# Routed experts by halves: tiles of one expert from scattered rows, expert matrices chosen by a register

## The chip, the cores and the metric

One core of a Trainium2 chip. The metric is the device time of one execution in microseconds (us). The engines are named as in the profile: PE is TensorE, DVE is VectorE, ACT is ScalarE, POOL is GpSimd, SP is SyncE, whose instructions here are nearly all DMA issues.

## The reference

A decoder of two layers on `x` of 4 x 256 tokens x 256, float32. Layer 0 is attention with 16 heads, a graph attention over a context, and 32 masked experts of which each token takes one. Layer 1 is attention with rotary positions (16 heads, 4 key heads of 128), a cross attention, and the stage that changes:

```python
probs = softmax(xt @ w_router)                     # xt: 1024 tokens x 256, 16 experts
top_w, top_i = top_k(probs, 4);  top_w /= sum(top_w)
cw = zeros(T, 16).at[arange(T)[:, None], top_i].add(top_w)
g = silu(einsum('td,edh->teh', xt, we1)) * einsum('td,edh->teh', xt, we3)    # h = 128
moe_out = einsum('teh,ehd->td', g * cw[:, :, None], we2)
shared = silu(xt @ ws1) * (xt @ ws3) @ ws2         # hidden size 512
out = shared / 5 + moe_out * 4 / 5
x = layernorm(x + out)
```

## The kernel before

Everything stays in SBUF between stages; each stage is a block with a hand-written instruction stream per engine, and semaphores between them. Every float32 product is made as three matmuls in fp32r: an operand is kept as a rounded part (`_hi`) and the rest (`_lo`), and `mm3` (L115) adds hi*hi, hi*lo and lo*hi in PSUM.

The last block, `cross_and_experts`, has the norm behind the attention, the cross attention, norm5, the turning of x into `xt_hi` and `xt_lo` (channels on partitions), the router, and then 20 "pieces": 16 experts and four quarters of the shared expert (`PIECES`), all dense: each piece is computed for all 1024 tokens, and VectorE adds its output to `c.x`, scaled by a gate per token that is 0 for an expert not chosen (`add`). For a piece, `up` does 24 matmuls with 512 moving columns (first and third matrix, two halves of the tokens), ScalarE takes silu, VectorE the product, ScalarE the rounded part and GpSimd the rest (`low`), and `down` does 24 matmuls with 256 moving columns for eight tiles of 128 tokens. `up` of the next piece stands before `down` of the present one. SyncE loads a piece's three matrices into two buffers in turn, and GpSimd splits them in two parts (`split`, L1682 and L1684). norm6 and four stores end the kernel.

Layer 0's masked experts (`graph_and_masked_experts`) already work by sorting: `rank` and VectorE's steps behind it give each token's place in an order by expert, eight indirect DMAs on GpSimd (L1380) scatter the rows of x to DRAM, SyncE loads them back, TensorE turns them and multiplies each tile of 64 rows with the matrix of its expert, whose column comes from a register (L1440, L1441), results go to DRAM by SyncE (L1358), and eight indirect DMAs gather them (L1388).

The diff also touches the attention block, which both layers use. In it SyncE's queue is one loop over the groups g of heads, which for layer 1 (`rope`) comes to: wait for the splits of the projections of group g - 1, load `raw_q` and `raw_k` of g; wait for the split of `raw_o` of g - 1, load `raw_o` of g. GpSimd splits these weights (L398, L401) and adds the two parts of the rotated queries and keys (`rotate`, L626), in an order written out by hand; TensorE waits for these sums before a step's scores (L759). In layer 0, behind the load of `raw_o` of group 2, SyncE also writes zeros to the 3 MB of `sorted_rows` (L600).

## Time and profile before

| what | us |
|---|---|
| median of 3 runs | 902.44 (900.88 to 908.67) |
| the profiled execution, its own time | 903.48 |
| its span, first to last instruction | 901.7 |

Mean granted clock of TensorE: 0.955 of full speed. Busy shares of the span: PE 89%, DVE 64%, ACT 48%, POOL 55%; 20% for the DMA queue of SyncE's transfers. Engines work at the same time, so a share says what an engine could still take, not what its work is worth; that is read from what others wait for. The times in the rows count from the first instruction of the span.

### The profile page before, as it was taken

What the parts mean: (1) busy time and instruction counts of PE and PEld (TensorE: products, weight loads), DVE (VectorE), ACT (ScalarE), POOL (GpSimd) and SP (SyncE); (2) the same over time, 40 slices, a digit from 0 to 9 for tenths busy, and PEclk for the clock granted to TensorE, in tenths of its full rate; (3) what the DMA queues carried; (4) which work ended last, traced back from release to release, by engine and by line L of the source; (5) the groups of instructions that cost most, each with busy time, mean ns of one, the idle gap of its engine ahead of it and who ended that gap; (6) DMA issues with size and microseconds to landing.
All of it is one profiled execution on the core that took longest, in us unless ns stands there. A gap on an engine that the chain in (4) does not pass through costs nothing. (4 is left out here: it accounts for less than half of the span.)

```text
span 901.7 us, 14551 instructions
## 1 busy us (share of the span) xinstructions
PE 801.8 (89%) x4733; PEld 685.0 (76%) x4733; DVE 574.4 (64%) x1651; ACT 429.2 (48%) x1209; POOL 499.8 (55%) x411
## 2 busy tenths in 40 slices
PE   7899999999999876792789999998987599999995
PEld 5678888888888764490678888887875388888885
DVE  4696867868769466123677667876736655545545
ACT  4264635536446544162366665666663532232232
POOL 4757287556587351513455564556422367777774
PEclk8999999999999997896999999999999799999998
DMA  6220711212315112553001111011001011111111
GB/s 200 71 94 1 234 36 59 94 36 106 115 50 180 55 54 65 186 120 88 30 6 48 53 53 53 1 54 53 24 1 37 12 35 52 35 52 52 35 41 47
DMA packets 58331, 59.09 MB, mean 66 GB/s; under 512 B 5392, under 2 KB 49312, under 8 KB 58272
## 3 DMA queue, kind: packets, MB, share of 16 engines
q1 hardware_dynamic: 57504, 56.24, 20.0%
q0 software_dynamic: 768, 2.10, 0.7%
q8 instruction: 32, 0.52, 0.2%
q14 instruction: 27, 0.22, 0.1%
HBM read 50.00 MB, written 8.32 MB: 65 GB/s over the span
## 5 line engine op out<-in xcount | busy, mean ns | idle before, releaser
L889 ACT ACTIVATE a_probs<-bank,a_neg_peak 128x128 f32<-128x128 f32 (+1 forms) x256 | 103.2, 429 | 88.9 <-DVE a_neg_peak L997 88.9
L917 ACT ACTIVATE a_probs<-a_probs,a_row_inv 128x128 f32<-128x128 f32 (+1 forms) x256 | 92.0, 447 | 20.8 <-DVE a_row_inv L1005 20.7
L997 DVE CUSTOM_DVE_ANT_0 bank<-bank,causal 128x128 f32<-128x128 f32 (+1 forms) x256 | 82.3, 394 | 15.3 <-PE bank L759 15.3
L895 ACT ACTIVATE a_probs_t<-bank 128x512 f32<-128x512 f32 x96 | 53.9, 597 | 73.5 <-PE bank L779 73.5
L1700 POOL TENSOR_TENSOR d_h_lo<-d_h,d_h_hi 128x512 fp32r<-128x512 f32 x40 | 51.7, 1293 | 52.6 <-ACT d_h_hi L1819 39.0
L398 POOL TENSOR_TENSOR a_wk_hi<-raw_k,one 128x512 fp32r<-128x512 f32 (+1 forms) x24 | 21.6, 901 | 102.3 <-DMA raw_k<-in_L_attn_w_k_dram 64.1
L798 PE MATMUL bank<-a_probs_t,a_vals 128*128 128x256 f32 x256 | 76.5, 380 | 0.0
L118 PE MATMUL bank<-a_wo_hi,a_ot_hi 128*128 128x256 f32 x256 | 74.5, 291 | 0.7 <-DVE a_ot_lo L1017 0.7
L1905 DVE TENSOR_TENSOR d_h<-d_silu,bank 128x512 f32<-128x512 f32 x40 | 27.5, 688 | 72.9 <-PE bank L120 72.8
L119 PE MATMUL bank<-a_wo_lo,a_ot_hi 128*128 128x256 f32 x256 | 73.2, 286 | 0.0
L120 PE MATMUL bank<-a_wo_hi,a_ot_lo 128*128 128x256 f32 x256 | 73.1, 286 | 0.0
L1912 DVE SCALAR_TENSOR_TENSOR x<-bank,d_gate,x 128x256 f32<-128x256 f32 x160 | 64.6, 477 | 2.5 <-PE bank L120 0.2
L140 PE MATMUL bank<-idle 128*128 128x512 bf16 x98 | 32.7, 505 | 35.3 <-DVE x L1597 16.3
L118 PE MATMUL bank<-xt_hi,d_w_hi 128*128 128x512 f32 x160 | 63.9, 400 | 0.0
L120 PE MATMUL bank<-xt_hi,d_w_lo 128*128 128x512 f32 x160 | 63.9, 399 | 0.0
L119 PE MATMUL bank<-xt_lo,d_w_hi 128*128 128x512 f32 x160 | 63.9, 399 | 0.0
L765 PE MATMUL bank<-a_keys,a_queries 128*128 128x256 f32 x256 | 60.6, 379 | 0.0
L779 PE MATMUL bank<-ident,a_probs 128*128 128x128 f32 x384 | 53.4, 275 | 6.2 <-ACT a_probs_t L895 6.2
L779 PEld LDWEIGHTS bank<-ident,a_probs 128*128 128x128 f32 x384 | 44.3, 141 | 16.5 <-ACT a_probs_t L895 10.8
L626 POOL TENSOR_TENSOR a_queries<-sim 128x512 f32<-128x512 f32 x32 | 40.7, 1279 | 27.6 <-DVE sim L972 27.6
L972 DVE TENSOR_TENSOR sim<-bank,a_sin 64x512 f32<-64x512 f32 x80 | 55.0, 688 | 1.1
L889 ACT ACTIVATION_READ_ACCUMULATOR a_probs<-bank,a_neg_peak 128x1 f32 x256 | 55.3, 216 | 0.0
(316 smaller groups left out, 2429.5 us busy)
## 6 DMA issues: line engine op xcount, KB each, us to landing
d_raw<-in_L_ffn_we_dram SPq DMA_DIRECT2D x48, 128.0 KB, 2.2
raw_k<-in_L_attn_w_k_dram SPq DMA_DIRECT2D x8, 512.0 KB, 6.5
raw_q<-in_L_attn_w_q_dram SPq DMA_DIRECT2D x8, 512.0 KB, 5.7
raw_v<-in_L_attn_w_v_dram SPq DMA_DIRECT2D x8, 512.0 KB, 7.3
raw_o<-in_L_attn_w_o_dram SPq DMA_DIRECT2D x8, 512.0 KB, 3.7
kv<-_L_ffn_expert_masks_dram SPq DMA_DIRECT2D x16, 256.0 KB, 3.1
kvt<-_L_ffn_expert_masks_dram SPq DMA_DIRECT2D x16, 256.0 KB, 3.1
raw_q<-in_L_attn_Wq_dram SPq DMA_DIRECT2D x8, 512.0 KB, 4.7
```

Source lines behind the costliest of these rows:

```text
L118: nc.tensor.matmul(out, l_hi, r_hi, start=start, stop=False)
L119: nc.tensor.matmul(out, l_hi, r_lo, start=False, stop=False)
L120: return nc.tensor.matmul(out, l_lo, r_hi, start=False, stop=stop)
L765: last = nc.tensor.matmul(out, queries[:, j, row + P:row + T], keys[:, j % keys.shape[1], row:row + width], start=True, stop=True)
L779: last = nc.tensor.transpose(c.banks[3 + turned % 2][:, slot % 4 * P:(slot % 4 + 1) * P], probs[s % 2][:, i, at:at + P], c.ident[:])
L798: nc.tensor.matmul(out, vals_of(s)[:, 2 * i, cols], probs_t[:, at:at + T], start=True, stop=False)
L889: nc.scalar.activation(probs[s % 2][:, i, at:at + width], c.banks[i][:, at:at + width], ACT.Exp, bias=neg_peak[:, n:n + 1], scale=-1.0, ac ...
L895: nc.scalar.activation(probs_t[:, i * BANK:(i + 1) * BANK], c.banks[3 + (3 * s + i) % 2][:], ACT.Copy).then_inc(s_pt_free, 1)
L917: last = nc.scalar.activation(part, part, ACT.Copy, scale=row_inv[:, s % 2, n + r:n + r + 1])
L972: last = nc.vector.tensor_tensor(two(across[to:to + HALF_BLOCK, n % 2]), two(bank[at:at + HALF_BLOCK]), many(sin[at:at + HALF_BLOCK], HALF ...
L997: last = nc.vector.tensor_tensor_reduce(part, part, mask, -1.0, 3e38, ALU.add, ALU.min, neg_peak[:, n + r:n + r + 1])
L1912: last = nc.vector.scalar_tensor_tensor(c.x[:, t], c.banks[4 + u][:, (t % 2) * D:(t % 2 + 1) * D], g, c.x[:, t], ALU.mult, ALU.add, accum_ ...
```

## The change

The routed experts become sparse; the shared ones stay dense.

- Tokens are taken in two halves of 512. For each half, the four chosen experts of each token give four places in an order by expert, in which each expert begins a new tile of 128 rows. `TILES1` = (512 x 4 - 16) // 128 + 16 = 31 is the most tiles that can be needed, and always all 31 are computed, in `PAIRS1` = 16 pairs (the last has one tile).
- `scatter`: GpSimd writes x's rows to `sorted1` in DRAM with 16 indirect DMAs for a half; `load_sorted`: SyncE loads pairs of tiles; `turn`, `hidden`, `turn_hidden`, `outputs` on TensorE; `sorted_high`, `silu_of`, `hidden_high`, `evict` on ScalarE; `sorted_low`, `gated`, `hidden_low` on VectorE. The expert's matrices stay in SBUF for all 16 experts (`w`), and a tile's are found by a register loaded from `column`. `store` writes results to `y_sorted`; `gather`: 16 indirect DMAs on GpSimd for a half; `combine`: VectorE adds the four rows of a token times their gates.
- All weights are split before the first routed product: ScalarE rounds (`high`), GpSimd or VectorE take the rest (`low`); several pieces are split ahead of the router. The shared experts run by halves (8 steps) while places are found and rows are scattered.
- In layer 1's attention SyncE writes zeros to `sorted1`: 2 MB behind the load of `raw_o` in each of the groups 1 to 4.
- Memory of earlier stages is given back for the expert matrices (`early`), and semaphores of the first two blocks are cleared and used again.

The diff, cut to its core:

```diff
@@ decoder
+        c.sorted1 = [nc.dram_tensor(f"sorted_rows1_{half}", (2 * PAIRS1 * P, D), F32, kind="Internal").ap() for half in range(2)]
@@ attention, SyncE's loop over g
                     weights.load(sp, "o", g)
...
+                    if rope and g <= 4:
+                        blank = c.idle[:].bitcast(F32).unsqueeze(1).broadcast_to([P, PAIRS1, D])
+                        rows = slice((g - 1) % 2 * PAIRS1 * P, ((g - 1) % 2 + 1) * PAIRS1 * P)
+                        sp.dma_start(c.sorted1[(g - 1) // 2][rows].rearrange("(t p) d -> p t d", p=P), blank).then_inc(c.s_blank, 16)
@@ graph_and_masked_experts, SyncE, at its start
+                for sem in c.finished:
+                    sp.sem_clear(sem)
@@ cross_and_experts
+TILES1 = (HALF * TOPK - EXPERTS1) // P + EXPERTS1
+PAIRS1 = -(-TILES1 // 2)
+    ORDER = ["s0", "s1", 0, 1, 2, "s2", "s3"] + list(range(3, EXPERTS1))
...
+                for n in range(len(Pieces.ORDER)):
+                    load_piece(n)
+                for i in range(8):
+                    load_sorted(i)
+                for i in range(ALL):
+                    if i + 8 < ALL:
+                        load_sorted(i + 8)
+                    store(i)
@@ GpSimd
+                def scatter(half):
+                    pool.wait_ge(s_place, half + 1)
+                    for t in HALF_TILES[half]:
+                        for k in range(TOPK):
+                            nc.gpsimd.indirect_dma_start(c.sorted1[half], bass.IndirectOffsetOnAxis(place[:, t, k:k + 1], 0), c.x[:, t], None).then_inc(s_scattered[half], 16)
+                def gather(t):
+                    if t % (NT // 2) == 0:
+                        for i in range(4):
+                            pool.wait_ge(s_stored[i], 16 * (PAIRS1 // 4) * (t // (NT // 2) + 1))
+                    if t >= 2:
+                        pool.wait_ge(s_summed, t - 1)
+                    for k in range(TOPK):
+                        nc.gpsimd.indirect_dma_start(got[t % 2][:, k], None, y_sorted[t // (NT // 2)], bass.IndirectOffsetOnAxis(place[:, t, k:k + 1], 0)).then_inc(s_got[t % 2], 16)
                 norm4.roots(pool)
+                low(0)
+                low(1)
...
+                for n in range(2, 5):
+                    low(n)
                 norm5.means(pool)
                 norm5.roots(pool)
-                split_up(0, 0)
-                with pool.Fori(0, PIECES // 2 - 1) as i:
...
+                pool.wait_ge(s_norm5, NT)
+                for n in range(5, 8):
+                    low(n)
+                pool.wait_ge(c.s_blank, 16 * 5)
+                scatter(0)
+                for n in pieces.by_pool[8:]:
+                    low(n)
+                scatter(1)
+                for t in HALF_TILES[0]:
+                    gather(t)
+                norm6.root(pool, 0)
+                for t in HALF_TILES[1]:
+                    gather(t)
+                norm6.root(pool, 1)
@@ TensorE
+                def hidden(i, columns):
+                    pe.wait_ge(s_xs_lo, i + 1)
...
+                        for k in range(KC):
+                            hi, lo = (w_flat[:, bass.ds(columns[2 * (i % 4) + t] + (j + k) * D, D)] for j in (0, 3))
+                            last = mm3(nc, out, xs_hi[:, i % 2, k, at], xs_lo[:, i % 2, k, at], hi, lo, k == 0, k == KC - 1)
-                turned5.pe(pe, s_norm5, 4)
-                router.pe(pe, turned5)
-                up(0, 0)
...
+                turned5.pe(pe, s_norm5, 4, halves=[0])
+                router.raw_pe(pe, turned5, halves=[0])
+                turned5.pe(pe, s_norm5, 4, halves=[1])
+                router.logits_pe(pe, halves=[0])
+                up(0)
+                rank(0)
...
+                for n in range(1, STEPS1):
+                    if n + 1 < STEPS1:
+                        up(n + 1)
+                    down(n)
+                turn(0)
+                turn(1)
+                split_wait(pe, len(Pieces.ORDER) - 1)
+                for i in range(ALL + 2):
+                    if i < ALL:
+                        if i % 4 == 0:
+                            columns[i // 4] = columns_of(i)
+                        hidden(i, columns[i // 4])
+                    if 1 <= i <= ALL:
+                        turn_hidden(i - 1)
+                    if i + 2 < ALL:
+                        turn(i + 2)
+                    if i >= 2:
+                        outputs(i - 2, columns[(i - 2) // 4])
@@ ScalarE
+                for n in range(STEPS1):
+                    shared(n)
+                    if n + 8 in pieces.by_dve:
+                        high(n + 8)
+                    shared_high(n)
+                for n in pieces.by_pool[8:]:
+                    high(n)
+                for half in range(2):
+                    act.wait_ge(s_above, half + 1)
+                    nc.scalar.activation(likely[:, part_of(half)], above[:, part_of(half)], ACT.Exp).then_inc(s_likely, 1)
+                nc.scalar.activation(primed[:], c.one[:], ACT.Silu)
+                sorted_high(0)
+                sorted_high(1)
@@ VectorE
+                norm5.apply(dve, 0, s_norm5)
+                turned5.dve(dve, halves=[0])
+                norm5.apply(dve, 1, s_norm5)
+                choose(0)
+                turned5.dve(dve, halves=[1])
+                find(0)
+                shared(0)
+                shared_low(0)
+                choose(1)
+                shared(1)
+                shared_low(1)
+                find(1)
+                for n in range(2, STEPS1):
+                    shared(n)
+                    for m in LOWS_AT[n]:
+                        low(m)
+                    shared_low(n)
+                    if n == SHARED:
+                        shared_total(0)
+                shared_total(1)
...
+                AT = {PAIRS1 + 5 + 2 * j: j for j in range(NT // 2)}
+                for i in range(ALL + 1):
+                    if i < ALL:
+                        gated(i)
+                    if i >= 1:
+                        hidden_low(i - 1)
+                    if i + 2 < ALL:
+                        sorted_low(i + 2)
+                    if i in (2, 4):
+                        gates(i // 2 - 1)
+                    if i in AT:
+                        combine(AT[i])
+                aggregate(0)
+                norm6.apply(dve, 0, s_norm6)
+                for t in HALF_TILES[1]:
+                    combine(t)
+                aggregate(1)
+                norm6.apply(dve, 1, s_norm6)
```

## Rows read from the trace of the kernel before

**Rows 1.** Windows by stage: length, busy us (instructions), granted clock, DMA share, GB/s

```profile
432.00:680.00 248.00, 228.79 (x1393) 199.87 (x1392) 168.37 (x480) 150.95 (x473) 125.57 (x98) 0.99 0.10 34
...
720.80:891.90 171.10, 171.08 (x962) 148.79 (x961) 94.83 (x235) 50.72 (x83) 119.24 (x117) 0.99 0.14 40
891.90:901.70 9.80, 0.00 (x0) 0.00 (x0) 4.22 (x16) 4.04 (x16) 2.83 (x6) 0.67 0.32 107
```

**Rows 2.** Chain of waits through one piece of the experts: start us, us, what

```profile
829.78 0.24 PE bank L118
...
838.25 0.24 PE bank L118
```

**Rows 3.** Timeline of TensorE, layer 0: start us, us, engine line op, idle

```profile
383.68 0.36 PE L1440 MATMUL bank<-b_w,xt_hi 128*64 x1
...
387.42 1.03 PE L1424 MATMUL bank<-ident,spare 128*128 128x128 f32 x8
```

**Rows 4.** Groups by line in the experts: busy us, mean ns, idle before

```profile
L1905 DVE TENSOR_TENSOR d_h<-d_silu,bank 128x512 f32<-128x512 f32 x40 | 27.5, 688 | 72.9 <-PE bank L120 72.8
L1684 POOL TENSOR_TENSOR d_w_lo<-d_raw,d_w_hi 128x512 fp32r<-128x512 f32 x20 | 25.8, 1292 | 1.6
...
L1816 ACT ACTIVATE d_silu<-bank 128x512 f32<-128x512 f32 x40 | 23.9, 597 | 54.6 <-PE bank L120 53.0
...
L1821 ACT ACT_TABLE_LOAD x1 | 1.3, 1283 | 0.0
```

**Rows 5.** Timeline of VectorE, norm5's scalings by halves

```profile
707.45 1.39 DVE L1183 TENSOR_SCALAR x<-x,d_d_norm_neg_mean,d_d_norm_rstd 128x256 f32<-128x256 f32 x4 [1.79 <-POOL d_d_norm_rstd L1167]
709.54 4.85 DVE L1183 TENSOR_SCALAR x<-x,d_d_norm_neg_mean,d_d_norm_rstd 128x256 f32<-128x256 f32 x4 [0.70 <-POOL d_d_norm_rstd L1167]
```

**Rows 6.** Timeline of VectorE, start of layer 0's finding

```profile
354.82 0.19 DVE L1557 TENSOR_SCALAR b_segments<-bank 128x32 f32<-128x32 f32 x1 [1.47 <-PE bank L1414]
```

**Rows 7.** Timelines of layer 0's indirect DMAs, 354 to 425 us

```profile
358.74 1.85 POOL L1380 DMA_INDIRECT sorted_rows<-x,b_place  x1 [16.98 <-DVE b_place L1572]
...
406.75 0.57 SPq L1358 DMA_DIRECT2D y_sorted<-raw_o  x1
...
410.27 1.01 POOL L1388 DMA_INDIRECT sim<-y_sorted,b_place  x1 [8.31 <-DMA y_sorted<-raw_o]
...
419.28 1.18 POOL L1388 DMA_INDIRECT sim<-y_sorted,b_place  x1 [0.30 <-issue]
...
422.25 0.43 DVE L1595 TENSOR_TENSOR sim<-sim,rows 128x256 f32<-128x256 f32 x1 [1.71 <-DMA sim<-y_sorted,b_place]
```

**Rows 8.** Timeline of SyncE's queue in layer 1's attention

```profile
471.72 0.37 SPq L383 DMA_DIRECT2D raw_o<-in_L_attn_Wo_dram  x1
...
472.68 0.47 SPq L383 DMA_DIRECT2D raw_k<-in_L_attn_Wk_dram  x1
```

**Rows 9.** Timeline of GpSimd in layer 1's attention, group 2's splits

```profile
477.16 0.61 POOL L398 TENSOR_TENSOR a_wk_hi<-raw_k,one 128x256 fp32r<-128x256 f32 x1 [5.46 <-DMA raw_k<-in_L_attn_Wk_dram]
...
480.78 2.54 POOL L626 TENSOR_TENSOR a_queries<-sim 128x512 f32<-128x512 f32 x2
```

**Rows 10.** Timeline of TensorE, the scores behind them

```profile
483.38 1.16 PE L759 MATMUL bank<-a_keys,a_queries 128*128 128x128 f32 x8 [0.19 <-POOL a_queries L626]
```

**Rows 11.** Timelines of SyncE and GpSimd, layer 0, loads behind its blank DMA

```profile
92.92 6.71 SPq L383 DMA_DIRECT2D raw_q<-in_L_attn_w_q_dram  x1
...
108.97 1.04 POOL L398 TENSOR_TENSOR a_wk_hi<-raw_k,one 128x512 fp32r<-128x512 f32 x1 [17.04 <-DMA raw_k<-in_L_attn_w_k_dram]
```

**Rows 12.** Window within that blank DMA, columns as in rows 1

```profile
96.00:98.00 2.00, 2.00 (x14) 1.76 (x13) 1.79 (x5) 0.60 (x1) 0.00 (x0) 1.00 1.08 386
```

**Rows 13.** Timelines of GpSimd and TensorE, layer 1, behind group 4

```profile
567.60 1.29 POOL L626 TENSOR_TENSOR a_queries<-sim 128x512 f32<-128x512 f32 x1 [1.98 <-DVE sim L972]
...
572.28 1.06 PE L759 MATMUL bank<-a_keys,a_queries 128*128 128x128 f32 x8
```

**Rows 14.** Window at half the granted clock, columns as in rows 1

```profile
722.00:724.00 2.00, 2.00 (x6) 1.63 (x5) 1.78 (x20) 1.55 (x2) 0.00 (x0) 0.50 0.00 0
```

More of the change, by code:

```diff
@@ new lines, in cross_and_experts @@
+        same = sb("same", [P, NT // 2, TOPK, EXPERTS1])
+        chosen = [sb(f"chosen{h}", [P, NT // 2 + 1, EXPERTS1], BF16) for h in range(2)]
+        earlier, every = sb("earlier", [P, P], BF16), sb("every", [P, P], BF16)
+        segments, through, ones = sb("segments", [P, EXPERTS1]), sb("through", [P, EXPERTS1]), sb("ones", [P, EXPERTS1])
+        magic, primed = sb("magic", [P, 2]), sb("primed", [P, 1])
+        tile_number, tile_expert = sb("tile_number", [1, EXPERTS0]), sb("tile_expert", [1, EXPERTS0])
@@ L1723, in _, with rank @@
+                norm6.root(pool, 0)
+                for t in HALF_TILES[1]:
+                    gather(t)
+                norm6.root(pool, 1)
             @block.tensor
             def _(pe):
-                pe.sem_inc(s_out, 2 * OUT)
-                pe.sem_inc(s_up, 8)
+                def rank(half):
+                    pe.wait_ge(s_chosen, half + 1)
+                    at = (NT + half * (NT // 2 + 1)) * EXPERTS1
+                    out = router.outs[half][:, at:at + (NT // 2 + 1) * EXPERTS1]
+                    nc.tensor.matmul(out, earlier[:], flat_of(chosen[half][:]), start=True, stop=False)
+                    for t in range(NT // 2):
+                        later = NT // 2 - t
+                        last = nc.tensor.matmul(out[:, (t + 1) * EXPERTS1:], every[:], chosen[half][:, t:t + 1].broadcast_to([P, later, EXPERTS1]), start=False, stop=t == NT // 2 - 1)
+                    last.then_inc(s_rank, 1)
@@ new lines, in down @@
+                def down(n):
+                    half, name, first = n // SHARED, f"s{n % SHARED}", n % SHARED == 0
+                    if first and half:
+                        pe.wait_ge(s_total, 2)
+                    for u in range(2):
+                        if first:
+                            nc.tensor.matmul(c.banks[2 + u][:], c.ident_bf[:], c.zero[:].broadcast_to([P, BANK]), start=True, stop=False)
+                        if u == 0:
+                            pe.wait_ge(s_h_lo, n + 1)
+                        for t in range(2):
+                            cols = slice((2 * u + t) * P, (2 * u + t + 1) * P)
+                            last = mm3(nc, c.banks[2 + u][:, t * D:(t + 1) * D], h_hi[:, n % 2, cols], h_lo[:, n % 2, cols], w_hi[name][:, KC], w_lo[name][:, KC],
+                                       False, t == 1 and n % SHARED == SHARED - 1)
+                        last.then_inc(s_shared, 1)
@@ new lines, in columns_of @@
+                def columns_of(i):
+                    if i % PAIRS1 == 0:
+                        pe.wait_ge(s_column, i // PAIRS1 + 1)
+                    first = i % PAIRS1 // 4 * 8
+                    _, columns = nc.values_load_multi_w_load_instructions(column[i // PAIRS1][0:1, first:first + 8], engines=[mybir.EngineType.PE], min_val=0, max_val=(EXPERTS1 - 1) * 2 * PIECE,
+                                                                          skip_runtime_bounds_check_because="VectorE counts at least 0 experts and takes at most the last")
+                    return columns
@@ L1856, in _ @@
                 for half in range(2):
[L1857 removed]
+                    part = part_of(half)
                     dve.wait_ge(s_exp, HALF_TILES[half].stop)
@@ L1864, in _ @@
                     last.then_inc(norm5.s_sum, 1)
-                for half in range(2):
-                    norm5.apply(dve, half, s_norm5)
-                turned5.dve(dve)
-                wide = lambda v: v.broadcast_to([P, NT, EXPERTS1])
-                dve.wait_ge(router.s_logits, 1)
-                nc.vector.tensor_copy(logits[:], router.out[:, 0:NT * EXPERTS1].rearrange("p (t e) -> p t e", t=NT))
-                dve.drain()
-                for t in range(NT):
-                    nc.vector.max(best[:, t], logits[:, t])
@@ L1876, in _ @@
-                dve.drain()
-                nc.vector.tensor_tensor(above[:], logits[:], wide(best[:, :, 0:1]), ALU.subtract).then_inc(s_above, 1)
-                nc.vector.memset(best[:, :, TOPK:], 3e38)
-                dve.drain()
-                for t in range(NT):
-                    nc.vector.match_replace(others[:, t], best[:, t], logits[:, t], -3e38)
-                dve.drain()
-                nc.vector.tensor_tensor(more[:], logits[:], others[:], ALU.is_gt)
-                dve.wait_ge(s_likely, 1)
```

604 lines of the change are left out of this document (398 added, 206 removed).

## The prediction

> **What bounds the kernel now.** I read the stretches by stage first [rows 1]. Layer 1's attention takes 248.0 us; norms, cross attention and router follow, then 171.1 us of dense experts and a tail of 9.8 us. TensorE is busy 171.08 of the 171.1 us with experts, so there its own work is the bound; in the attention it is busy 228.8 of 248 and every small gap matters. The second view is the chain in the experts [rows 2]: one piece (an expert, or a quarter of the shared one) begins at 829.78 and the next at 838.25, a period of 8.47 us. In it a 512-column matmul costs 0.233 us (the steps of 0.24, 0.23, 0.23 in the chain), so a 256-column one (8.47 - 24 x 0.233)/24 = 0.12 us. A matmul's own row shows 0.28 or more, which is latency, since they overlap. Twenty pieces at 8.47 make 169 us, the stage. DMA is lightly used (40 GB/s). Third, for a part of the diff that lies outside the experts, the timelines of GpSimd, SyncE and TensorE in layer 1's attention.
>
> **Fewer tile products.** Now 16 experts x 8 tiles of 128 tokens = 128 products; each is 18432/8 = 2304 columns. The new code always does 31 tiles in each half, so 62 products of nine 256-column matmuls (2304 columns too), whatever the router says. New for each tile: three 128x128 transposes (two of the rows, one of the hidden layer). Layer 0 already works like this with registers: 32 matmuls with a register in the address run from 383.68 to 387.42, 0.117 each, and eight transposes take 1.03 with the latency of the last, so about 0.11 each; nothing is left there for the loading of eight registers [rows 3]. I take 0.119 and 0.11: 62 x 9 x 0.119 = 66.4, 62 x 3 x 0.11 = 20.5, together 87 us where 16 x 8.47 = 135.5 stood: 48.6 us less on TensorE. For two tiles ScalarE does two 256-column copies or activations and two of 512 (some 2.0 us by its 0.60 for 512 columns [rows 4]), VectorE some 1.6 us by its 0.69 [rows 4], against TensorE's 2.8, so TensorE still leads.
>
> **The start of the experts.** Now TensorE reaches its first expert matmul at 720.84. Before it, VectorE needs 4.85 us for the four scalings of norm5's second half where the first took 1.39, while GpSimd splits weights [rows 5]. The change makes GpSimd wait for norm5 and orders the work by halves: second half scaled some 711.6 to 713.0, transposes to 714, first-half logits 715. So the shared experts start at 715, 5.8 earlier. For this I take GpSimd's three lows (1.9 us each, by 1.29 for 512 columns [rows 4]) and ScalarE's highs (0.85 each) as hidden in the stretch where TensorE does nothing anyway; if they meet the two tiny VectorE scalings behind the peaks, it costs up to 4.
>
> **The shared experts, halves and finding.** Eight steps of 12 wide and 12 narrow matmuls: 12 x 0.233 + 12 x 0.119 = 4.2 us, 34 us. But choosing and finding stand on VectorE ahead of the first two products. Layer 0's finding began at 354.82 [rows 6], and its first scatter, released by the places, at 358.74 [rows 7]; by halves some 2.8, choosing 2.5, and the experts' numbers behind each place 2.0. Walked through in order this gives down(0) at 729.5, rank(1) at 732, down(2) at 741.3 and the last product's end at 762.2: 47 us. Then ScalarE has four weight copies (3.5), two table loads of 1.28 [rows 4] and two 512-column copies, and GpSimd four lows (7.8); the first routed product starts at 768.7, 6.5 us idle. Scatter of half 0: 16 issues at the 1.29 us of layer 0's indirect DMAs (410.27 to 419.28 is seven of them [rows 7]), 21 us from 725, hidden under the shared experts (without that cover it would cost all 20); that of half 1 lies under half 0's products: it ends at about 790. Two queues stand behind it: SyncE waits for it before loading half 1's rows, with the stores of results 8 and later queued behind that wait (first needed at 797, when the twelfth copy reuses its buffer), and TensorE reaches half 1 at 813. VectorE waits in its order for each gather of half 0 before later tiles' products; that is priced below.
>
> The Trainium skill, page "SBUF — State Buffer", section "SBUF: two separate sides", speaks against this: VectorE operations with two SBUF inputs can hold the port that GpSimd needs, and its descriptors starve. Rows show little of it for indirect DMAs (1.01 us alone, 1.18 beside VectorE's two-input sums [rows 7]). By the rule the eight lows of weights (1.0 us each) and eight of hidden rows (0.7) on VectorE, 13.6 us, would move the scatter's end from 746 to about 760, still ahead of 768.7, so the sum would not change.
>
> **Routed phase.** 87 us, plus 2 for a slow clock after the idle time, 2 to fill and drain the pipeline, 4 where VectorE waits for half 0's gathers (bounds 0 and 12: the first gather lands about where its sum stands in the order, and each gather of four takes 5.2 against 5.6 for two steps). Bounds for all three: 2 and 18. TensorE ends at 768.7 + 95 = 863.7, where it now ends at 891.9.
>
> **The tail.** Now 9.8 us. New, after the last matmul: copy and wait 0.8; store issued to first gather 3.5 (406.75 to 410.27 [rows 7]); 16 gathers, 15 x 1.29 = 19.3 to the last issue; landing 2.9 (419.28 to 422.25 [rows 7]); four sums 2.0; moments 1.2; root 1.6; scaling 1.4; store 2.9. Sum 35.6. GpSimd reaches half 1's gathers only behind norm6's first root, which waits for VectorE's aggregate, but that is over before the last store lands; a gather also waits for the sum of the tile two before (9 us after that tile's first issue, where 10.3 us of issues lie between). So the end is at 899.3 against 901.7: the experts by themselves give **2.4 us**. The 48.6 us of TensorE go into 13 for the shared experts' latency, 6.5 for the gap, 8 for the pipeline and 26 for the tail, with 6 back at the start.
>
> **The blank DMAs in the attention.** The diff makes SyncE write 2 MB of zeros (16 x 128 rows of 1 KB) behind the load of raw_o in groups 1 to 4 of layer 1's attention. On SyncE's queue the very next instructions are the loads of raw_q and raw_k for the next group: raw_o is issued at 471.72, raw_q directly behind and raw_k at 472.68 [rows 8]. And GpSimd stands waiting for that raw_k: 5.46 us idle to 477.16, splits, then at once the two rotations of the queries until 483.3 [rows 9]. TensorE's next scores start at 483.38, 0.19 us after it had run dry, released by exactly these queries [rows 10]. So raw_k's landing lies on the chain to TensorE, with no slack. Layer 0 shows what a blank ahead of loads does: 3 MB issued just before raw_q's load at 92.92, SyncE stuck 6.71 us in issuing raw_q, raw_k landed at 108.97, GpSimd idle 17.04 us [rows 11], while DMA ran at 386 GB/s [rows 12]. 2.1 MB at 386 GB/s is 5.4 us; layer 0's raw_k was 2.7 us later than the bytes ahead of it need (raw_o, blank, raw_q and raw_k are 4.7 MB, 12.2 us; counted from 94.0, 1.1 us behind raw_q's issue), so up to 7.2 here. I take 6. Groups 1 to 3: 3 x 6 = 18. In group 4 the rotation now waits 1.98 us for VectorE and TensorE for nothing [rows 13]: the splits would end at 571.6 instead of 565.6, two rotations at 574.15, TensorE starts 1.9 after its 572.28. Together 20 us (bounds 17.5 and 24.7). What is late next is TensorE itself, busy from there on; nothing gives the time back. After idle stretches of 4.5 us the clock's record is at half for some 3 us (0.50 at 722 to 724, in the middle of busy experts, some 8 us after the idle time that ended at 714.4 [rows 14]), where TensorE does half the work: 1.5 to 2 lost each, bounds 0 and 9 for the three, I take 6. Sum **26 us**.
>
> Costed at nothing: the clearing of some forty semaphores on SyncE, which has 22 us to wait there for TensorE's transposes; the loops written out as straight code (bounds -1 to 3, since more instructions must be fetched); 25 MB more DMA traffic below the experts (some 190 GB/s where the experts have 40 and the engines reach 386).
>
> Against the profiled execution (903.48; span 901.7 and 1.8 outside): 903.5 - 2.4 + 26 = 927.1. It was 1.0 above the median of 902.44, so 926.1; I say **926**.
>
> **Rivals.** (a) *The blanks are absorbed*, a gain being possible. For it: in layer 0 the same kind of DMA left TensorE fully busy (2.00 of 2.00 at 96 to 98 [rows 12]). Against: there TensorE did not wait on the next split. It decides by the wait in front of the scores: if it stays under 1 us, the time is 902.4 - 2.4 = 900. With the experts' terms at their cheap ends (start of routed 4 earlier, pipeline 6 less, tail 3 less) it is 887, **faster**: the rival of the other sign, decided by whether raw_k still lands near 477. (b) *The delay is there, but the experts gain as much*: shared phase at 40 instead of 47 and the cheap ends above, 926 - 20 = 906. (c) *Indirect DMAs are the bound*: if they cost 2 us each instead of 1.29, the tail grows by 11 and VectorE waits 9 more in the routed phase: 946. For it: the first scatter in layer 0 took 1.85 [rows 7]; against: the gathers took 1.01 to 1.18. (d) *The work is not halved*: 62 is fixed in the code, so this can't fail by the router's choices.
>
> **Chances.** Forecast 0.63, its own range 912 to 940; (a) near 900 0.12, (a) at the cheap end 0.08; (b) 0.09; (c) 0.08. Changes under 1% are about what a measurement of this kernel can't tell from none (893.4 to 911.5). Faster 0.10, same 0.20, slower 0.70. The range takes in (b) and half of (a): 898 to 941.
>
> **What would show it.** Waits of GpSimd for raw_k of 11 us instead of 5.5 in groups 1 to 4, and gaps of 5 to 7 us on TensorE before the scores of groups 1 to 3, 2 in the fourth; attention about 26 longer. From the end of attention on: first expert matmul some 35 us after it, last matmul some 183 after it, last gather issue 23 after that. It would be wrong if the loads overtake the blanks, if fine-grained steps leave TensorE idle between routed products (over 0.3 us each), or if scatter 0 outlasts the shared experts.

## The result and the profile after

The changed kernel took **955.53 us** (median, 954.01 to 956.52) against 903.91 for the kernel before, a ratio of 1.0565 (95%: 1.0513 to 1.0616). Slower, as forecast, but 29.5 us beyond the 926 and outside the range of 898 to 941. The profiled execution took 956.52, its span is 954.7. The three stretches that answer to [rows 1], TensorE's windows by stage (length; busy time and instructions of each engine; clock; DMA share; GB/s):

```profile
core 0: us, PE busy (x) PEld busy (x) DVE busy (x) ACT busy (x) POOL busy (x), PEclk, DMA share, GB/s
462.00:711.00 249.00, 210.61 (x1266) 185.97 (x1266) 146.87 (x421) 136.74 (x424) 111.64 (x86) 0.95 0.20 65
748.00:917.40 169.40, 141.90 (x970) 130.83 (x970) 91.18 (x236) 80.55 (x165) 60.43 (x56) 0.90 0.51 157
917.40:954.70 37.30, 0.00 (x0) 0.00 (x0) 12.65 (x32) 0.38 (x1) 17.80 (x19) 0.54 0.33 99
```

The first window holds only the last 249 us of an attention that ends at 710.99; TensorE, busy 228.8 of 248 before, is busy 210.6 here. The expert stretch, 171.08 of 171.1 busy before, has 27.5 us without work. The tail is 37.3 us.

**Attention.** The timeline of SyncE and GpSimd at the first group's end, and TensorE's first scores of the next four groups (start, duration, engine, line; in brackets the idle time before it and what ended it), which answer to [rows 8 to 10]:

```profile
470.33 0.37 SPq L394 DMA_DIRECT2D raw_o<-in_L_attn_Wo_dram  x1
470.74 0.51 SPq L615 DMA_DIRECT2D sorted_rows<-idle  x1
471.29 3.83 SPq L394 DMA_DIRECT2D raw_q<-in_L_attn_Wq_dram  x1
475.16 1.09 SPq L394 DMA_DIRECT2D raw_k<-in_L_attn_Wk_dram  x1
...
482.69 0.61 POOL L409 TENSOR_TENSOR a_wk_hi<-raw_k,one 128x256 fp32r<-128x256 f32 x1 [12.39 <-DMA raw_k<-in_L_attn_Wk_dram]
...
488.81 1.01 PE L774 MATMUL bank<-a_keys,a_queries 128*128 128x128 f32 x3 [7.00 <-POOL a_queries L641]
...
525.53 0.80 PE L774 MATMUL bank<-a_keys,a_queries 128*128 128x128 f32 x2 [6.66 <-POOL a_queries L641]
...
563.77 1.01 PE L774 MATMUL bank<-a_keys,a_queries 128*128 128x128 f32 x3 [7.79 <-POOL a_queries L641]
...
600.90 1.16 PE L774 MATMUL bank<-a_keys,a_queries 128*128 128x128 f32 x8 [2.26 <-POOL a_queries L641]
```

The blank goes first, the issue of raw_q's load is stuck 3.83 us behind it, raw_k lands late and GpSimd waits 12.39 us for it instead of 5.46; TensorE runs dry for 7 us instead of 0.19. The forecast chain, link by link. From the first raw_o issue to the end the attention takes 240.7 us (470.33 to 710.99) against 208.5: 32 more. Its price was forecast at 26.

**A hole that no step of mine had.** TensorE, ScalarE, VectorE, GpSimd and SyncE in the middle of the routed phase:

```profile
810.12 0.38 ACT L2026 ACTIVATE xt_hi<-bank 128x256 fp32r<-128x256 f32 x1 [1.05 <-PE bank L1913]
810.54 0.42 DVE L2201 TENSOR_TENSOR xt_lo<-bank,xt_hi 128x256 fp32r<-128x256 f32 x1 [1.01 <-ACT xt_hi L2026]
...
812.33 0.41 PE L131 MATMUL bank<-d_w,xt_lo 128*128 x1
812.67 0.96 POOL L1798 DMA_INDIRECT sorted_rows<-x,d_place  x1 [0.30 <-issue]
813.94 0.96 POOL L1798 DMA_INDIRECT sorted_rows<-x,d_place  x1 [0.30 <-issue]
815.04 0.36 SPq L1764 DMA_DIRECT2D d_scratch<-sorted_rows  x1
815.05 0.60 ACT L2011 ACTIVATE xt_hi<-bank 128x512 fp32r<-128x512 f32 x1 [4.54 <-issue]
815.20 0.96 POOL L1798 DMA_INDIRECT sorted_rows<-x,d_place  x1 [0.30 <-issue]
815.68 0.69 DVE L2188 TENSOR_TENSOR xt_lo<-bank,xt_hi 128x512 fp32r<-128x512 f32 x1 [4.72 <-issue]
...
816.51 0.58 PE L129 MATMUL bank<-d_w,xt_hi 128*128 x1 [3.76 <-issue]
```

I call this a hole. Three engines stand for 3.8 to 4.7 us and start within 1.5 us of each other; none names a releaser ("issue"), and TensorE stops between two tiles of one pair, where the code has no wait. Only GpSimd goes on, with an indirect DMA every 1.26 us: the scatter of half 1. SyncE's loads of sorted rows issue in the same jerks. Two more such groups of holes, at 873 to 880 and 887 to 900, go with the gathers of half 0. From the first routed product (800.29) to TensorE's end (917.4) it takes 117 us; forecast were 95.

### The profile page after: what moved, and what is told of

Its sections match the earlier page's. It is cut to its first block and busy times, and to the rows that moved or that the text cites. A ratio compares the mean times of both kernels' runs of the same rounds, so it can differ in the third digit from the quotient of the medians.

```text
span 954.7 us, 14582 instructions
## 1 busy us (share of the span) xinstructions
PE 777.7 (81%) x4723; PEld 671.4 (70%) x4723; DVE 574.0 (60%) x1674; ACT 460.4 (48%) x1281; POOL 461.3 (48%) x365
## 5 line engine op out<-in xcount | busy, mean ns | idle before, releaser
L129 PE MATMUL bank<-d_w,xt_hi 128*128 x186 | 60.2, 323 | 12.5 <-issue 6.6
L774 PE MATMUL bank<-a_keys,a_queries 128*128 128x128 f32 x256 | 39.0, 300 | 34.3 <-POOL a_queries L641 32.0
L780 PE MATMUL bank<-a_keys,a_queries 128*128 128x256 f32 x256 | 65.7, 403 | 0.0
L1807 POOL DMA_INDIRECT d_scratch<-y_sorted,d_place x32 | 30.8, 963 | 65.7 <-DMA y_sorted<-kvt 49.8
L774 PEld LDWEIGHTS bank<-a_keys,a_queries 128*128 128x128 f32 x256 | 34.5, 208 | 38.1 <-POOL a_queries L641 34.8
L130 PE MATMUL bank<-d_w,xt_hi 128*128 x186 | 55.8, 300 | 1.0 <-issue 1.0
L131 PE MATMUL bank<-d_w,xt_lo 128*128 x186 | 56.1, 301 | 0.0
L780 PEld LDWEIGHTS bank<-a_keys,a_queries 128*128 128x128 f32 x256 | 50.1, 206 | 6.3
```

The source lines that it names most:

```text
L129: nc.tensor.matmul(out, l_hi, r_hi, start=start, stop=False)
L130: nc.tensor.matmul(out, l_hi, r_lo, start=False, stop=False)
L131: return nc.tensor.matmul(out, l_lo, r_hi, start=False, stop=stop)
L774: last = nc.tensor.matmul(c.banks[i][:, at:at + width], queries[:, j, row:row + P], keys[:, j % keys.shape[1], row:row + width], start=Tru ...
L780: last = nc.tensor.matmul(out, queries[:, j, row + P:row + T], keys[:, j % keys.shape[1], row:row + width], start=True, stop=True)
```

## The experiments

Each is given with its median, that of the kernel before on the same chip, and the ratio with its 95% interval. They ran on six chips, and where they ran turned out to matter; which chip the first measurement had is not known. Each chip was used on one occasion only, so "a chip with holes" below means a chip as it was on that occasion: no run tells the chip itself from whatever else belonged to the occasion.

**1. The blanks behind the loads.** In SyncE's loop:

```diff
+ load q, k of group g
+ if rope and g <= 4: 2 MB blank
  wait for the o splits; load o
- if rope and g <= 4: 2 MB blank
```

> The changed kernel with one thing moved: each 2 MB blank is issued behind the q and k loads of its group and no longer behind the o load, so the next thing behind it is an o load that is needed only at the group's end. Theory A (the blanks ahead of the next group's q and k loads are the whole cost of attention, some 9 us in each of three groups and 2.5 in the fourth): attention from the first o load to its end comes back to 208.5 us from 240.7, the raw_k idle on GpSimd to about 5.5 us from 12, and the kernel to 925 (920 to 930). Rival B (the transfers slow attention wherever they lie, through the DMA engines or the memory): periods of 33 to 37 us in the first three groups stay, time 945 or more. Rival C (the start of the expert block pays for it): the same gain in attention, and less than 25 us in all.

Measured: **900.31**, before 901.78, ratio 0.9978 (0.9944 to 1.0011). SyncE and GpSimd there:

```profile
466.42 0.51 SPq L394 DMA_DIRECT2D raw_q<-in_L_attn_Wq_dram  x1
466.97 0.47 SPq L394 DMA_DIRECT2D raw_k<-in_L_attn_Wk_dram  x1
467.48 0.47 SPq L601 DMA_DIRECT2D sorted_rows<-idle  x1
...
472.46 0.61 POOL L409 TENSOR_TENSOR a_wk_hi<-raw_k,one 128x256 fp32r<-128x256 f32 x1 [6.48 <-DMA raw_k<-in_L_attn_Wk_dram]
```

The same 8 MB now cost 1 us a group: GpSimd waits 6.48 for raw_k, and the periods of the first three groups are 29.0 to 29.3 against 28.0 to 28.4 before. From the first raw_o issue to the end of attention it takes 214.4, so 6 of the 32 us stay. The 1 us isn't firm either: in five of the nine traces with late blanks, that of the same kernel in experiment 9 among them, the first group pays more, with raw_k 3 us later and periods of 31.0 to 34.2:

```profile
478.02 0.61 POOL L409 TENSOR_TENSOR a_wk_hi<-raw_k,one 128x256 fp32r<-128x256 f32 x1 [8.79 <-DMA raw_k<-in_L_attn_Wk_dram]
```

Theory A's mechanism holds, but the time is 25 us below its 925: the experts, untouched, take 217.5 us from their first SyncE instruction (680.4) to the end instead of 243.7.

**2. The blanks alone, on the kernel before.**

```diff
+ if rope and g <= 4: 2 MB blank, behind the load of o
```

> The kernel before with the four 2 MB blanks alone, where the change has them; its results don't use them. Theory A: the attention part of the change is the blanks, so this is 32 us over the kernel before, 936 (931 to 940), with periods of 37 us in the first three groups. The rival, that the renamed and released semaphores, the tiles allocated later or the code itself also slow attention, gives less than 25 us over the kernel before, and the rest would have to come from elsewhere.

Measured: **932.19**, before 901.78, ratio 1.0330 (1.0276 to 1.0385): 30.4 us. First raw_o issue to the end of attention 238.6 (473.8 to 712.4), periods 37.5, 36.9, 37.9 and 34.5 (before 28.0, 28.4, 28.2, 32.2). So 30 of the 32 are the blanks. The rest lies behind the last raw_o issue, where most traces of the new code take 35.6 to 36.8 and this one 34.1 as before; but the kernel of experiment 3, without the new code, took 36.8 there too, so that stretch varies and isn't shown to be of the change.

**3. Half the size.** The same with blanks of 1 MB.

> The kernel before with the four blanks at half their size, 1 MB each (half of the scattered rows' buffer is left out; its results don't use it). At full size they cost 30.4 us. If the stall is the transfer time ahead of the q and k loads, each of the first three groups loses 2.7 us less (1.05 MB at 386 GB/s) and the fourth loses nothing: 20 us, 921 to 924. Rival: a slack behind the loads hides the first part, so half the size costs under 10 us (912 or less). Rival: the cost hangs on the stall's being there at all (the granted clock falls and takes the same time to come back), 25 us or more (927 up).

Measured: **921.64**, before 902.27, ratio 1.0209 (1.0177 to 1.0241): 19.4 us, as forecast. GpSimd's wait for the first raw_k, at full and at half size:

```profile
486.84 0.61 POOL L399 TENSOR_TENSOR a_wk_hi<-raw_k,one 128x256 fp32r<-128x256 f32 x1 [13.12 <-DMA raw_k<-in_L_attn_Wk_dram]
```
```profile
477.84 0.61 POOL L399 TENSOR_TENSOR a_wk_hi<-raw_k,one 128x256 fp32r<-128x256 f32 x1 [9.72 <-DMA raw_k<-in_L_attn_Wk_dram]
```

3.4 us less for 1 MB less (2.7 to 4.3 over the four groups), so no slack hides a first part, and the fourth group's period is 32.2 as before: there the delay (9.29 instead of 5.67) fits in what it had to spare.

**4. Without the second scatter.**

```diff
- scatter(1)
- SyncE: wait for s_scattered[1]
```

> The changed kernel without the 16 indirect DMAs that scatter half 1 (half 1's rows are left blank: the expert products run on zeros, as many as before). Theory T1 (while GpSimd's indirect DMAs run, all engines stand still on nothing that the profile names, because what they fetch and what SyncE issues over the DMA queues waits): the hole at 807 to 823 goes, with the half clock behind it, the routed phase shortens by 9 to 13 us from 117 and the time is 943 to 947; the holes at 873 to 880 and 887 to 900, which go with gathers, stay. Rival T2 (straight-line code is fetched too slowly at the start of the routed phase, whatever the DMAs do): the hole stays, time 953 to 957. Rival T3 (VectorE or ScalarE was late with the first tiles): the waits on xt_lo and rows stay, time over 950.

Measured: **926.89**, before 901.78, ratio 1.0269 (1.0214 to 1.0324). Half 1's products run on blank rows here. Below every theory's figure: the hole is gone, but so are those with the gathers, which had been left alone.

**5. Part of the second scatter earlier.**

```diff
  scatter(0)
+ scatter(1), the first 9 of its 16 indirect DMAs
  the last four low parts
- scatter(1)
+ scatter(1), the other 7
```

> The changed kernel with 9 of the 16 indirect DMAs of half 1's scatter issued right behind those of half 0, in the 12 us in which GpSimd waits before the last four low parts (779 to 791); 7 stay where they are. Under T1 the burst in the routed phase ends at about 807 instead of 818, so the hole there shrinks to a few us: 946 to 950; something may be given back in the shared phase, where the products are twice as long and fewer instructions are fetched. Under T2 and T3 no change: 953 to 957.

Measured: **929.09**, ratio 1.0310 (1.0255 to 1.0364), again with no hole at all. Experiments 1, 4 and 5 are different edits, and each lacks some 26 us; what they share is the chip they ran on.

**6. The changed kernel again, with 1 and late gathers beside it.**

> The changed kernel as it is, once more and beside other kernels on one chip: in the three runs before this one, which left its routed code as it is or only moved scatters, no hole in the routed phase was left (TensorE's end 179 to 180 us after the experts' start instead of 206), in one of them with every indirect DMA at the same place. Theory P (the holes belong to this program as it is laid out: where its code or its tensors lie): 953 to 957 again, with holes at about 97 to 112, 162 and 183 us after the experts' start. Theory Q (the holes belong to the chip or the loading on which it ran): 927 to 932 here, with no holes, so 26 us of the 52 over the kernel before were not of the change.

> The kernel with the blanks behind the q and k loads, once more on the same chip as the changed kernel. Under P 898 to 902 as before. Under Q it stays 30 us below the changed kernel, whatever that has here.

Measured: the changed kernel **928.12**, before 902.41, ratio 1.0274 (1.0212 to 1.0336); the late blanks 901.25, ratio 0.9983 (0.9953 to 1.0013). This fits Theory Q: with nothing changed, the routed phase has no holes here. The same windows by stage of this run:

```profile
748.00:889.90 141.90, 131.27 (x971) 122.91 (x971) 90.44 (x236) 81.16 (x164) 60.36 (x56) 0.98 0.60 187
889.90:927.40 37.50, 0.03 (x1) 0.00 (x0) 12.64 (x32) 0.44 (x2) 17.94 (x20) 0.54 0.33 99
```

As many instructions, 27.5 us sooner done. DMA by queue in the 17 us under the second scatter (kind: packets, MB, share of 16 engines), first the first measurement (806 to 823), then this one (805.5 to 822.5):

```profile
q0 software_dynamic: 576, 1.57, 25.6%
q1 hardware_dynamic: 485, 0.46, 8.9%
```
```profile
q1 hardware_dynamic: 2987, 2.88, 56.6%
q0 software_dynamic: 529, 1.44, 23.1%
```

GpSimd's indirect DMAs (software) keep their pace in both; SyncE's (hardware) move a sixth in the first. That isn't a queue held back: in the first SyncE issued two loads in this window, in the second twelve loads and stores. The load issued inside the hole, at 815.04, is served at once. Its packets, in the window from 815 to 817.5 and in that from 808.4 to 822.4:

```profile
q1 hardware_dynamic: 272, 0.26, 31.9%
```
```profile
q1 hardware_dynamic: 272, 0.26, 5.7%
```

So all it moved in those 14 us it moved within 2.5 us of the issue, and none of it is seen waiting in the DMA engines, which were busy a third of the 17 us. What is late is the issuing of instructions, on SyncE as on the other three. The window from 808.4 to 822.4 has no packet of the instruction queues either, though all four engines went on within it: no fetched instructions are seen to end the hole.

The two traces differ in one more way. All 16 indirect DMAs of the first scatter have a recorded landing in the second (2.4 to 4.5 us) and none in the first; of 346 DMA issues, 273 have one against 123. It is so throughout: 111 to 185 in the seven traces with holes, 263 or more in the ten without, from the experts' first loads on, ahead of any hole.

The late gathers put half 0's gathers behind the last store:

```diff
- wait for the stores of this half
+ wait for the stores of both halves
- combine(0..3) between the products of half 1
+ combine(0..3) behind them
```

> The changed kernel with the gathers and sums of half 0 put off until every result of half 1 is stored. Their 16 indirect DMAs then lie behind TensorE's end: the tail grows from 37 to 37 + 20 (16 x 1.26) = 57 us. If the holes belong to the bursts of gathers, 2 to 6 us of routed phase come back, 968 to 974 (942 to 950 if the changed kernel has 928 here).

Measured: **956.57**, ratio 1.0571 (1.0499 to 1.0642), on the chip without holes, 6.6 over the 942 to 950 expected there. The tail is 65.9 us instead of 37.5: the hiding is worth 28, not 20, since sums, moments and scaling of half 0 come behind it too.

**7. Another chip.**

> The changed kernel once more, on whatever chip comes. The first measurement gave 955.5 with holes in the routed phase, the second, on another chip, 928.1 with none. If the holes are rare (Q), 926 to 932 again; 953 to 957 if they come with some chips or loadings.

Measured: **952.03**, before 902.27, ratio 1.0545 (1.0505 to 1.0585), and the holes are back: TensorE's end 202 us after the experts' start. The kernel before has the same time on all of them (medians 901.8 to 903.9). What separates the runs with holes from those without may be the chip or the occasion.

**8. Which burst opens which hole.** The kernels of 4 and 6 on a fourth chip.

> The changed kernel without the scatter of half 1 (half 1's products run on blank rows) again. Four measurements of the changed kernel so far: 955.5 and 952.0 with holes in the routed phase, on two occasions, and 928.1 (and its variants in line with it) on two other chips with none. Theory S (on some chips the hardware queues and the instruction fetch get nothing while GpSimd's indirect DMAs are under way): on such a chip the holes between 97 and 112 us after the experts' start go and those with the gathers stay: 938 to 944, and the late-gathers kernel beside it shows the first hole and not the others. On the other chips 925 to 932. Rival S2 (on such a chip the routed phase stalls at its start whatever GpSimd does): the first hole stays there, 948 or more.

> The changed kernel with the gathers of half 0 behind the last store, again. Under S on a chip with holes: the holes at 162 to 185 us after the experts' start go, those at 97 to 112 stay; 955 + 20 for the tail grown + 8 for what the tail had grown already on the other chip, less 8 for the holes: 972 to 980. On a chip without holes 950 to 958 as before.

Measured: **944.55**, ratio 1.0474 (1.0419 to 1.0528), and **974.99**, ratio 1.0805 (1.0752 to 1.0858), before 903.09: a chip with holes, the first 0.6 over Theory S's figures and the second inside them. Windows under the second scatter's place and under the gathers' place; first the kernel without the scatter, then that with late gathers:

```profile
803.00:827.00 24.00, 21.87 (x161) 21.47 (x160) 14.05 (x38) 13.44 (x29) 1.91 (x2) 0.82 0.45 140
868.00:892.00 24.00, 19.47 (x137) 18.36 (x138) 15.22 (x33) 10.70 (x24) 9.21 (x10) 0.86 0.59 179
```
```profile
803.00:827.00 24.00, 13.65 (x74) 12.59 (x75) 5.30 (x10) 4.60 (x12) 14.85 (x16) 0.64 0.38 122
868.00:892.00 24.00, 24.00 (x207) 24.00 (x206) 12.37 (x26) 15.34 (x35) 0.00 (x0) 1.00 0.55 177
```

Where GpSimd has no indirect DMA, TensorE is busy 24.00 of 24.00 with 207 matmuls; under the scatter, 13.65 with 74. (In the kernel without the scatter the first window holds the wait before the first routed product, at 805.73.) Each burst opens its own holes. On this chip the shared phase is longer too: the first routed product comes 94.1 and 93.5 us after the experts' start, where it was 89.3 in the first measurement. That is 5 us lost during and just behind the first scatter, which no run takes apart.

**9. Gathers spaced out.** On top of experiment 1:

```diff
  gather(t), for each k:
+   if t is of half 0: wait for one more output pair of TensorE
    indirect DMA
- combine(0..3) every second pair from pair 21
+ combine(0..2) at pairs 24, 28, 32, combine(3) behind them
```

> The kernel with the blanks behind the q and k loads, a third time, as the base of the three beside it. On a chip without holes 898 to 902 as twice before; on a chip with holes 952 less 28 = 922 to 928.

> The same base, with the 16 gathers of half 0 spread over the products of half 1: each waits for one more output pair of TensorE, 2.8 us apart instead of 1.26, and the sums are put behind them. On a chip with holes, if it is the density of the indirect DMAs that keeps the hardware queues out, the holes with the gathers go: 5 to 8 us less than the base. If each indirect DMA costs the others the same wherever it lies, no difference over 2 us. On a chip without holes within 2 us of the base.

Measured on a chip without holes: base 901.89, paced 907.43, before 903.57, ratio 1.0055 (1.0023 to 1.0087): 5.5 more, more than the 2 expected; the sums now trail into the tail, 45.2 us there. It said nothing about density, so it ran again:

> The kernel with late blanks and paced gathers again, one more chip. On a chip with holes its own trace answers: there the scatter of half 1 opens its hole at about 97 to 112 us after the experts' start. If density is what counts, the stretch with the paced gathers has no hole of 1 us or more on TensorE; if each indirect DMA blocks by itself, some 5 us of holes are spread over it. On a chip without holes 905 to 912 as before, and the question stays open.

Measured: **921.86**, before 903.93, ratio 1.0201 (1.0090 to 1.0313, from two runs), on a chip with holes. The windows under the scatter, 1.26 us between indirect DMAs, and under the gathers, 2.8 us between most of them:

```profile
770.00:796.00 26.00, 13.10 (x78) 11.85 (x78) 3.85 (x7) 6.49 (x13) 18.91 (x19) 0.74 0.44 144
826.00:882.00 56.00, 53.01 (x445) 52.22 (x443) 33.58 (x74) 35.30 (x80) 15.17 (x16) 1.00 0.66 199
```

In the second window TensorE has its last product at 879.2, so it is idle 0.2 us in all; in the first it is idle for half the time. So 16 indirect DMAs spaced out open no hole in a run in which 16 close together do, while gathers 1.25 us apart had opened holes in the first measurement and in experiment 7: their density counts. One thing stays uncompared, the dense gathers on this same chip. And the total isn't shown to gain: the tail is 45.0 us as on the chip without holes, and there was no base beside it.

**10. Scatter in the gap, with late blanks.** The edit of 5 on 1.

> The same base, with 9 of the 16 indirect DMAs of half 1's scatter moved out of the routed phase into GpSimd's wait before it. On a chip with holes: if what counts is that they lie beside the routed products, which come at 25 matmuls in 2.8 us, the first hole shrinks and 5 to 9 us are won, less what the shared phase loses; if they cost as much beside the shared products, nothing is won, or the last loads of weights come late and it is worse. On a chip without holes within 2 us of the base.

Measured: 902.52, ratio 0.9986 (0.9951 to 1.0021): no difference to the base, on a chip without holes. On one with holes it wasn't run.

**11. The first routed product sooner.** On top of experiment 1:

```diff
  VectorE: low parts 8 to 15 at shared steps
- 8 | 9,10 | 11 | 12,13 | 14 | 15   (steps 2 to 7)
+ 8,9 | 10,11 | 12,13 | 14,15       (steps 2 to 5)
  ScalarE: high parts two to a step in steps 1 to 6
- likely exponentials, then the first two high parts of sorted rows
+ the high parts first
  SyncE: load_sorted(0..3) ahead of the last two pieces
```

> The kernel with the blanks behind the q and k loads, and the gate in front of the first routed product moved forward: VectorE's low parts 8 to 15 two to a shared step from the second on, ScalarE's high parts two to a step from 1 to 6, the first four loads of sorted rows ahead of the last two expert pieces, and the two table loads with the gate exponentials behind the first two high parts of sorted rows. Theory G (the last low parts on GpSimd gate the first routed product, 88.5 us after the experts' start, while the shared experts end at 81.5): first routed product at 84 to 85, everything behind it earlier by as much, 4 us in all: 896 to 897, 0.994 of the kernel before. Rival: the loads of the pieces are late for the earlier slots, ScalarE waits for them in front of the shared chain, and the shared phase gets longer by what is won: 899 to 902.

> The kernel with the blanks behind the loads and the low parts earlier, again. On a chip with holes 919 to 927 as before, where the first routed product came no sooner (89.1 us). On a chip without, theory G gives 896 to 897 and the first routed product at 84 to 85 us; its rival 899 to 902.

> The version with the low parts earlier, a third time (923.2 and 927.5 on chips with holes). On a chip without holes theory G gives 4 us under the base, 896 to 897; its rival, that the shared phase gives it back, the base's time within 1 us. On a chip with holes the base's time within 3 us, since the first routed product came no sooner there.

Measured: 923.22, before 902.27 (1.0242, 1.0202 to 1.0282) and 927.46, before 903.09 (1.0260, 1.0209 to 1.0311), on chips with holes; **899.20**, before 903.57 (0.9958, 0.9935 to 0.9982), on one without. The last is under 1%. And theory G fell there: the first routed product comes 89.7 us after the experts' start (base 87.7), its last wait now short:

```profile
768.20 0.38 PE L129 MATMUL bank<-d_w,xt_hi 128*128 x1 [1.06 <-DVE xt_lo L2190]
```

The gate moved, and the shared steps, waiting for VectorE behind its extra low parts, gave it back: their last product ends at 87.8 instead of 81.0. The experts take 216.2 us, the base 215.9. So the 2.7 us to the base aren't from there; in the two traces the difference lies ahead of the experts, in attention and before it.

## Why the forecast went as it did

The direction was right, and so was the mechanism in attention. Where there are no holes the size was too, 928.1 against 926, but partly by luck: attention cost 5 us more than forecast and the experts 3 less. The 955.5 that was to be forecast has holes in it that no step of mine held. By steps, with the profile of 928.1 (span 927.4) for those that holes don't touch:

- **The blanks, 26.** They are 30.4 by themselves (experiment 2); the whole attention is 32 longer. The stalls on TensorE (7.00, 6.66, 7.79 and 2.26) are 23.7, near the top of the 17.5 to 24.7; I had taken 6 us a group by the bytes, and raw_k was 6.9 us later. The rest, some 8, fits the slow clock, near its upper bound of 9: behind the three long stalls TensorE works for 4.6, 5.5 and 4.7 us at 0.50 (488.8 to 493.4, 525.5 to 531, 563.8 to 568.5), which costs 7.4. This term was mis-sized: layer 0's own figure, "up to 7.2", stood in the text, and I took less.
- **Start of the experts, 34.8 after the attention.** 38.0. The norm's first scaling already comes 3.2 us later than before (30.4 after the attention instead of 27.2), and the two tiny scalings behind the peaks take 0.55 and 0.61 instead of 0.17. So some of the "up to 4" for GpSimd's low parts and ScalarE's high parts was due; how much no run takes apart.
- **Shared experts to 82, first routed product 88.5.** 81.2 and 87.7: 43.2 us for the shared experts instead of 47.
- **Routed phase, 95.** 91.0 without holes (87.7 to 178.7): of the 8 for clock, filling and gathers, 4 were needed. With holes 117.1. This is **the step that failed**: "Costed at nothing: the loops written out as straight code (...); 25 MB more DMA traffic below the experts", beside bursts of 16 indirect DMAs on a queue of their own. I had priced those bursts by what GpSimd needs for them and by who waits for their data, and never by what they take from others. TensorE's waits from the first routed product on sum to 16.1 us, without holes to 0.6; the other 10 or so of the 26 fit the stretches in and behind the holes where it is busy at a clock of 0.50: 10.7, 3.3 and 6.1 us (811 to 828, 879.2 to 882.5, 896.3 to 903), worth 10. Experiments 8 and 9 show in its place that each burst of indirect DMAs costs such holes where they occur; the term was 26 us, not 0.
- **Tail, 35.6.** 37.5.
- Sum without holes: +31.0 for the attention, 216.2 for the experts instead of 221.5 (-5.3), together 25.7, the difference of the spans; forecast were 26 and -2.4. (The forecast's own account of TensorE's 48.6 us adds up to 1.1 and not 2.4, since twenty pieces of 8.47 are 169.4 and the stage is 171.1; the sum that gave the time doesn't use it.)
- **Rivals.** The blanks were not absorbed (a), the experts gained 5.3 and not 22 (b), indirect DMAs kept 1.26 us (c), and the work was halved (d). (c) had the right place, the indirect DMAs, but the wrong victim: they were on time themselves.
- The Trainium skill's rule on the port between VectorE and GpSimd (page "SBUF — State Buffer", section "SBUF: two separate sides") showed a little of itself: single indirect DMAs of 1.4 to 1.5 us instead of 0.96 in the first scatter, beside VectorE's two-input operations. The scatter took 22.7 us where 16 at 1.26 are 20.2, and that moved the sum by nothing.

Open: what holds the engines up. That it is instruction fetch was argued from four engines stopping together inside straight code with no releaser; no run shows it, and the record of the instruction queues doesn't speak for it. GpSimd runs straight code too and goes on. A rival stands untested: since the traces with holes also lack landings, the taking of the records itself may have a part, and no run tells. Open as well is whether the chip or the occasion decides.

## What to carry to other kernels

A filler transfer costs what it weighs if it is issued just ahead of a load that somebody is waiting for, and much less one instruction later (1 us a group, in some traces 3 to 6 in the first): look at who is next on the queue, not at how idle the DMA engines are. A burst of back-to-back indirect DMAs beside dense work is a risk that one chip may not show. Spaced by the progress of the engine that has the work they opened no holes, but the sums behind them came later, 5.5 us in all where there were no holes to save. Measure on more than one chip and occasion before a few per cent are believed. And this expert phase with half the matmuls gave back 43 of its 48 us, since scatter, finding, half-wise order and a bare gather tail went in front and behind it.

## What the hardware showed unexpectedly

- The same program takes 955.5, 952.0 or 928.1 us, by the chip or the occasion, while the kernel before stays within 901.8 to 903.9 (medians). Of the six chips of the experiments three have holes (7, 8 and the second run of 9) and three have none.
- On the ones with holes, TensorE, ScalarE, VectorE and SyncE stand together for some 4 us under indirect DMAs 1.26 us apart; under those 2.8 us apart TensorE has no wait over 0.2 us. The hardware queue moved 0.46 MB in 17 us, where 2.88 MB went through on another, because little was issued to it: the load issued within the hole was through in 2.5 us. The Trainium skill (page "DMA: Bandwidth & Descriptors", section "SWDGE vs HWDGE vs iDMA") has each DMA engine take its software and hardware queues in turn; the traces agree, with holes and without.
- A DMA of zeros delays a load behind it by somewhat more than its bytes: 3.3 us for 1 MB on the mean of four groups (2.7 to 4.3), where 386 GB/s would need 2.7.
